# An attention accumulator that is begun by the first output projection of a batch instead of being filled beforehand

## The reference, cut to what matters

```python
z = softmax(q @ k.T / 8) @ v          # per batch and head
z = concat_heads(z) @ w_o
x = layernorm(x + (x + z))            # so 2 * x + z is what is normalised
x = layernorm(x + (x + moe(x)))
```

## Time and profile before

| | |
|---|---|
| median of 3 runs | 1209.61 us (1207.98 to 1209.96) |
| the profiled execution | 1211.91 us |
| its span, first to last instruction | 1209.8 us |
| mean granted TensorE clock | 0.975 |

### The profile page before, as it was taken

The page is one execution under the profiler, slowest core; times in us unless marked ns, Lnnn a source line. Parts: engine busy times, 40 slices in busy tenths (PEclk is TensorE's granted clock), DMA queues, the critical chain, the costliest instruction groups (busy, mean ns, idle before and its releaser), DMA issues. The chain is left out here.

```text
span 1209.8 us, 18157 instructions
## 1 busy us (share of the span) xinstructions
PE 1099.0 (91%) x5912; PEld 669.2 (55%) x5912; DVE 783.4 (65%) x1106; ACT 615.8 (51%) x744; POOL 646.6 (53%) x313
## 2 busy tenths in 40 slices
PE   4898999999999999999999999999976888998886
PEld 2555555555555555555555555555534666776664
DVE  4665866666666666666666666666635567676864
ACT  3554655455545555455445554555442566655553
POOL 0465555545554555445544554455543566666655
PEclk9998999999999999999999999999997889999999
DMA  7111100100010001001000100100000000000000
GB/s 156 44 29 43 36 20 27 37 18 18 26 36 18 18 26 36 18 18 35 27 18 18 35 27 18 35 19 27 19 28 27 10 0 18 19 18 17 9 9 18
DMA packets 49430, 32.50 MB, mean 27 GB/s; under 512 B 28400, under 2 KB 38640, under 8 KB 49392
## 3 DMA queue, kind: packets, MB, share of 16 engines
q1 hardware_dynamic: 49392, 32.01, 9.1%
HBM read 23.07 MB, written 2.36 MB: 21 GB/s over the span
## 5 line engine op out<-in xcount | busy, mean ns | idle before, releaser
L987 DVE TENSOR_REDUCE neg_max<-psum 128x2 fp32r<-128x1024 f32 x256 | 313.8, 1226 | 119.9 <-PE psum L510 119.8
L541 PE MATMUL psum<-q_pair,k_pair 64*128 64x512 f32 x1536 | 227.0, 400 | 1.5 <-DVE xT L965 1.5
L399 POOL TENSOR_TENSOR k_pair<-x_tok,q_pair 128x1024 fp32r<-128x1024 f32 x64 | 152.2, 2388 | 92.0 <-ACT q_pair L926 92.0
L373 POOL TENSOR_TENSOR probs_sum<-x_tok 128x1024 f32<-128x1024 f32 x32 | 76.8, 2400 | 218.1 <-ACT x_tok L826 218.1
L373 POOL TENSOR_TENSOR probs_sum<-probs_even 128x1024 f32<-128x1024 f32 x32 | 76.7, 2396 | 201.3 <-ACT probs_even L826 201.3
L541 PEld LDWEIGHTS psum<-q_pair,k_pair 64*128 64x128 f32 x1536 | 140.0, 184 | 50.5 <-ACT probs_even L826 11.7
L833 ACT ACTIVATE sums<-psum 128x512 f32<-128x512 f32 x64 | 38.3, 598 | 243.2 <-PE psum L575 243.2
L373 POOL TENSOR_TENSOR probs_sum<-probs_sum,probs_even 128x1024 f32<-128x1024 f32 x64 | 152.7, 2386 | 6.1
L826 ACT ACTIVATE probs_even<-psum 128x1024 f32<-128x1024 f32 x128 | 128.3, 1026 | 53.4 <-PE psum L547 48.8
L373 POOL TENSOR_TENSOR probs_sum<-probs_sum,x_tok 128x1024 f32<-128x1024 f32 x64 | 152.1, 2377 | 6.1
L826 ACT ACTIVATE x_tok<-psum 128x1024 f32<-128x1024 f32 x128 | 128.1, 1025 | 50.7 <-PE psum L547 46.8
(11 more groups left out here) (116 smaller groups left out, 1667.2 us busy)
## 6 DMA issues: line engine op xcount, KB each, us to landing
recip<-recip_scratch SPq DMA_DIRECT2D x128, 128.0 KB, 2.8
xT_cur<-xT SPq DMA_DIRECT2D x8, 512.0 KB, 2.9
x_tok<-L_attn_x_dram SPq DMA_DIRECT2D x8, 256.0 KB, 5.3
sums_flat<-sums SPq DMA_DIRECT2D x128, 2.0 KB, 1.7
probs_even<-acc SPq DMA_DIRECT2D x8, 256.0 KB, 2.4
out_dram<-probs_even SPq DMA_DIRECT2D x8, 256.0 KB, 2.3
acc<-L_ffn_w_dram SPq DMA_DIRECT2D x1, 1024.0 KB, 5.5
recip_scratch<-recip_flat SPq DMA_DIRECT2D x64, 4.0 KB, 1.4
```

The costliest lines, as they stand in the source:

```text
L373: nc.gpsimd.tensor_tensor(probs_sum[:], left, probs[j][:, :, c, :], ALU.add).then_inc(s["added"], 1)
L399: nc.gpsimd.tensor_tensor(g_lo[e % GB], gated[e % 2], bits(g_hi[e % GB]), ALU.subtract).then_inc(s["g_lo_done"], 1)
L541: nc.tensor.matmul(psum[:, 2 * (t % 2) + h, :], k_pair[j][rows, kp, keys], q_pair[j][rows, qp, :], start=(kp == 1), stop=False)
L987: nc.vector.tensor_reduce(neg_max[:, :, t], psum[:, COARSE:COARSE + 2, :], AX.X, ALU.max, negate=True).then_inc(s["max_done"], 1)
```

## The change

`acc` is no longer filled. The first `acc_part` of a batch (hp = 0) becomes a scalar_tensor_tensor that writes 2 x high part + projection into `acc`, reading `xT` from SBUF and the projection from PSUM. The low part comes with a new operation, `acc_lo_part`: 2 x low part + `acc`, both read from SBUF, written to `acc`. It stands in DVE's list once per batch, in the body of hp = 2 right behind `acc_part` of pair (b, 0), ahead of the reciprocals and of maxima 2, and waits for that `acc_part`. The second `acc_part` of the batch (hp = 1, one body later) waits for `acc_lo`. The four `double`, the four `double_late` and the four L1075 are gone, with `late_sequences` and the semaphores `acc_set`, `acc_half`, `acc_late`. The transposes of batches 4 to 7 wait for `xT_hi_done` and `xT_lo_done` instead. The waits for the freed raw weights (`w_split`, `experts_split`) move to the first `acc_part` of a batch.

```diff
             def transpose_x(b):
-                wait(pe, s["acc_set"], b - 3)
+                wait(pe, s["xT_hi_done"], b - 3)
+                wait(pe, s["xT_lo_done"], b - 3)
...
-            def double(b):
-                act.wait_ge(s["xT_lo_done"], b + 1)
-                act.wait_ge(s["w_split"], b * 4 // B + 1)
-                nc.scalar.activation(acc[:, b, :], psum[:, b % 4, :], ACT.Copy, scale=2.0).then_inc(s["acc_set"], 1)
...
-            def double_late(b):
-                act.wait_ge(s["experts_split"], 3 if b < 3 * B // 4 else 4)
-                nc.scalar.activation(acc[:, b, :], bits(xT[:, b, 0, :]), ACT.Copy, scale=2.0).then_inc(s["acc_half"], 1)
...
             def acc_part(b, hp):
                 n = pair(b, hp)
                 dve.wait_ge(s["wo_done"], n + 1)
-                wait(dve, s["acc_done"], n)
-                if is_first(n):
-                    dve.wait_ge(s["acc_set"], B // 2)
-                if not isinstance(n, int):
-                    dve.wait_ge(s["acc_late"], B // 2)
                 a = acc[:, b, :]
-                nc.vector.tensor_tensor(a, psum[:, MISC, :], a, ALU.add).then_inc(s["acc_done"], 1)
+                if hp == 0:
+                    dve.wait_ge(s["w_split"], 4)
+                    if not is_first(n):
+                        dve.wait_ge(s["experts_split"], 4)
+                    nc.vector.scalar_tensor_tensor(a, bits(xT[:, b, 0, :]), 2.0, psum[:, MISC, :], ALU.mult,
+                                                   ALU.add).then_inc(s["acc_done"], 1)
+                else:
+                    wait(dve, s["acc_done"], n)
+                    if hp == 1:
+                        wait_apart(dve, (s["acc_lo"], b + 1))
+                    nc.vector.tensor_tensor(a, psum[:, MISC, :], a, ALU.add).then_inc(s["acc_done"], 1)
+
+            def acc_lo_part(b):
+                wait_apart(dve, (s["acc_done"], b * HP + 1))
+                a = acc[:, b, :]
+                nc.vector.scalar_tensor_tensor(a, bits(xT[:, b, 1, :]), 2.0, a, ALU.mult,
+                                               ALU.add).then_inc(s["acc_lo"], 1)
...
                 if before_former:
                     acc_part(*shifted_pair(b, hp, -2))
+                    if hp == 2:
+                        acc_lo_part(b)
...
-                for late in late_sequences(n):
-                    dve.wait_ge(s["acc_half"], late - B // 2 + 1)
-                    nc.vector.scalar_tensor_tensor(acc[:, late, :], bits(xT[:, late, 1, :]), 2.0, acc[:, late, :], ALU.mult,
-                                                   ALU.add).then_inc(s["acc_late"], 1)
```

More of the change, by code:

```diff
@@ L148, in attention_moe_kernel @@
         names = """x0_in x_near_in x_far_in w_in ident_set ones_set zeroed w_split gate_split
-            xT_done xT_hi_done xT_lo_done acc_set acc_half acc_late
+            xT_done xT_hi_done xT_lo_done acc_lo
             xT_cur_in
@@ L207, in chunks @@
             body(B - 1, 1)
[L209 to L213, removed]
         def expert_quarter(step):
@@ L847, in _ @@
             xT_part(2)
-            double(0)
             q_part(1, 1)
             xT_part(3)
-            double(1)
             k_part(1, 1)
-            double(2)
-            double(3)
             for k in range(2, 4):
@@ L877, in body @@
                     q_part(n + 2, hp + 2)
-                for late in late_sequences(n):
-                    double_late(late)
                 if not is_last(n, 2):
```

## The result

The changed kernel takes 1227.74 us (median of 4 runs, 1224.62 to 1229.02) against 1209.78 for the kernel before in the same comparison: a ratio of 1.0147, 95% interval 1.0124 to 1.017, so 15 to 21 us slower. The forecast was 1227.9. Both intervals hold +15, the first at its lower edge, and 14.9 and 15.0 are what the eight bodies with the new operation add up to in the two traces.

What follows compares the result with a forecast made beforehand. The attention runs at PE's pace (96% busy), with a recurring wait of coarse step 3 for maxima 2. 12.2 (waits) + 6.3 (clock) - 0.2 (removed) = +18.3 on the median 1209.61 gives 1227.9 us, range 1219 to 1240.

Steps and rivals of the forecast that it cites:

- The hold: Attention, hp = 2 bodies: new operation waits out POOL's addition, maxima 2 and coarse step 3 1.53 late, +12.2 us in all.
- the rival in which POOL's additions get in first: Same place: POOL's next two additions also precede the new operation, maxima 2 6.45 late; +51.4 us, 1261; chance 0.03.
- The clock: Attention, behind coarse step 3's longer gaps: PE's clock drops in 2.3 of eight batches at 2.7 us each, +6.3 us.
- The rival in which the clock holds: Attention: PE's clock does not fall at gaps of 1.93; +12.0 us, 1221.6; chance 0.20.
- a straight line over the length of the gap: Drop share per batch, interpolated between gaps of 1.61 (no drop) and 2.70 (drop): 0.29 at the forecast gap of 1.93.
- What was removed: ACT operations at the start, ACT and DVE operations late in batch 0: 0.2 us gained, bounds nothing to 7.3.
- The sum: Whole kernel: 12.2 waiting + 6.3 clock - 0.2 removed = +18.3 us, giving 1227.9.
- The bound from below: New operation runs unhindered in 0.68, maxima 2 0.21 late, 1.7 us for eight; as a rival +1.5, 1211.1, chance 0.08.

Runs made afterwards that it cites:

- the PSUM variant: Changed kernel, new operation in its place but reading a PSUM bank times 0 instead of the low part: 1211.36 us, ratio 1.0005 to the kernel before.
- the variant in which POOL waits: Changed kernel, but in bodies with hp = 2 POOL's first addition waits until the new operation is done: 1213.7 us, ratio 1.0029 to the kernel before.
- the one at the end of the body: Changed kernel, new operation moved behind diag in the same body instead of ahead of the reciprocals: 1209.92 us, ratio 0.9994 to the kernel before.
- the doubled operation: Changed kernel, new operation done twice in a row, each adding the low part once: 1259.65 us, ratio 1.0405 to the kernel before.
- the filled gap: Changed kernel, PE does six needless matmuls ahead of coarse step 3 in bodies with hp = 2: 1221.9 us, ratio 1.0095 to the kernel before.
- the second comparison: The changed kernel unaltered, measured again beside the kernel before: 1225.74 us, ratio 1.0124 (1.0107 to 1.014).

## Why the prediction was right, step by step

**The hold.** Right in mechanism and size. The new operation ended 0.56 after POOL's addition (0.55 forecast), took about 1.8 to 2.2 (2.0 forecast), maxima 2 came 1.53 late (1.53) and coarse step 3 waited 1.87 to 1.99 (1.93). Only POOL's next additions were held less than was said, 0.31 and not 0.55, and nobody waited for them. The excess of the eight bodies without the clock's share is 12.0 (12.2). That it is the second SBUF input and POOL's addition was argued from two rows; the PSUM variant, the variant in which POOL waits and the one at the end of the body each take away one condition, and each takes all or nearly all of the loss away (1.8 and 2.5 are left with the first two, nothing that can be measured with the third). The one-turn rule (one POOL operation waited out, then DVE's turn) is what the doubled operation shows; with it falls the rival in which POOL's additions get in first. In the five profiles in which the operation with two SBUF inputs met a POOL addition, all 48 of them ended 0.55 to 0.56 after that addition. The rule of the Trainium skill (SBUF — State Buffer, section Who interferes with whom), that on VectorE an instruction with two SBUF inputs contends with GpSimd's reads of SBUF and one with a single SBUF input, outside some modes, does not, agrees with the runs: 1.77 to 2.24 in its place with two, 0.69 there with one. That whoever issues first keeps the port for the whole instruction, this page of the Trainium skill says of other modes of VectorE; that an operation with two SBUF inputs waits for the end of POOL's addition is what these runs show.

**The clock.** Right in kind, near in number by luck, wrong in price. Forecast were 2.3 drops of 2.7, measured 2 of 1.5. The term that was mis-sized is the price: it came from pair 4, where the clock was low for 6.8 us; behind the new gaps it was low for 3.4. For 6.8 us the 2.7 was right: with the operation at the end of the body pair 4 had nearly the same gap (2.65) and no drop, and its body lasted 16.89 against 19.79, 2.9 less. The number came from a straight line over the length of the gap, which does not hold (see the last section), so that it lay near is chance. The rival in which the clock holds is refuted by the two low stretches and by the filled gap. The Trainium skill's advice (TensorE: Matmul & The Clock Gate, section Why this matters for your kernels), which warns of longer idle gaps only, would have let the clock hold; a gap of 1.88 lowered it here.

**What was removed.** Forecast -0.2; the kernel without the new operation measures 0.9993, that is -0.8 with an interval of -2.3 to +0.5, which neither shows nor excludes it. The start and the second phase are unchanged, as forecast.

**The sum.** The terms as measured are 12.0 + 3.0 = 15.0 against 18.3. The first median, 18.0 above before, sits closer to the forecast than its terms do: the second comparison gives 15.0, and the intervals of the two overlap between +15.0 and +16.9. So part of the agreement to 0.2 us is chance, and the prediction's clock term, 6.3, was twice too large.

**The bound from below** (unhindered, 1.7 for eight) was a good price too: with one input from PSUM, where nothing holds the operation, the bodies lost 1.8 in all.

## What to carry to other kernels

Before an operation is put into an engine's list, look at what the other engines do at that moment: the same operation cost nothing 6 us later and 1.5 us of TensorE's time here. A maximum in a row of durations that stands far from its median (2845 beside 683) is worth following up: what it waited for there is the price if the new place looks alike, here the end of POOL's addition and 0.55 more, not the 2845 itself. On VectorE, an operation that must run beside a GpSimd addition was cheaper here with one input from PSUM (0.69) than with two from SBUF (1.77 to 2.24).

## What the runs showed that was not expected

The price of a clock drop depends on how long the clock stays low, and that was not fixed by the size of the gap: gaps of 4.6 to 4.7 were followed by 3.4 us at 1.2 GHz in some batches and by 6.8 in others, gaps of 1.9 to 2.0 by none in six batches of eight, and one of 2.65, in pair 4 of the kernel with the operation at the end of the body, by none either:

```profile
97.15 0.49 PE L505 MATMUL psum<-k_pair,q_pair 64*128 64x512 f32 x2 [2.65 <-DVE neg_max L964]
97.58 0.50 PE L446 MATMUL psum<-xT,w_tab 128*128 128x512 f32 x1
97.91 0.39 PE L447 MATMUL psum<-xT,w_tab 128*128 128x512 f32 x1
```

(The projection behind it takes 0.39, where it takes 0.63 at 1.2 GHz.) So the length of a gap alone, on which the prediction drew its straight line, doesn't decide.

The load of the second expert weights, 1 MB in front of a 2 KB transfer on the same queue, cost the kernel before 5 us in one body, more than the interval leaves for what the change removes (2.3 at most).

That body is also a large part of what makes one execution differ from another. In the nine profiled executions that issue the load ahead of the reciprocal's transfers, the gap of pair 4 was 2.44 to 3.93 and the clock behind it was low for 6.8, for 3.4 or for no time, so the body lasted from 16.89 to 21.03. Two spans can differ by 4 us through it alone; what a change is worth is therefore read body by body.
